# Second layer's V in nine products instead of twelve, with the keys of a pair's first batch rotated

## The reference

```python
def _L1_xattn_ref(x, context, Wq, Wk, Wv, Wk_ip, Wv_ip, Wo, bo):
    HEADS, DIM_HEAD, TEXT_LEN, IMG_SCALE = 16, 64, 77, 1.0
    ctx_txt = context[:, :TEXT_LEN, :]
    ctx_img = context[:, TEXT_LEN:, :]
    q = (x @ Wq).reshape(B, N, HEADS, DIM_HEAD)
    k = (ctx_txt @ Wk).reshape(B, TEXT_LEN, HEADS, DIM_HEAD)
    v = (ctx_txt @ Wv).reshape(B, TEXT_LEN, HEADS, DIM_HEAD)
    out = _attend(q, k, v)
    k_ip = (ctx_img @ Wk_ip).reshape(B, Li, HEADS, DIM_HEAD)
    v_ip = (ctx_img @ Wv_ip).reshape(B, Li, HEADS, DIM_HEAD)
    out_ip = _attend(q, k_ip, v_ip)
    out = out + IMG_SCALE * out_ip
    return out @ Wo + bo
```

## Time and profile before

| | us |
|---|---|
| median of 3 runs | 666.07 (665.52 to 667.85) |
| profiled execution | 668.6 |
| its span in the trace | 666.9 |
| TensorE busy | 612.9 |
| VectorE busy | 492.2 |
| ScalarE busy | 464.8 |
| GpSimd busy | 308.2 |

### The profile page before, as it was taken

How to read it: one execution, slowest core, us unless ns; L and a number is a source line. 1 busy time by engine, 2 the same in 40 slices (tenths; PEclk the granted TensorE clock), 3 DMA queues, 4 the chain that set the end, 5 groups by cost and what they waited for, 6 DMA issues and landing times.

```text
span 666.9 us, 16387 instructions
## 1 busy us (share of the span) xinstructions
PE 612.9 (92%) x5665; PEld 560.3 (84%) x5665; DVE 492.2 (74%) x1255; ACT 464.8 (70%) x1347; POOL 308.2 (46%) x444
## 2 busy tenths in 40 slices
PE   5898999999999999999999999999999879989990
PEld 5787888988889899999989988888888868979990
DVE  6588787798887978888797986876655665656654
ACT  5987889988888896666666766667555354646762
POOL 4365344444444434354445343445265574456450
PEclk9998999999999999999999999999889798989995
DMA  9800000000000000336664020000000032112215
GB/s 221 260 2 1 1 1 1 2 2 2 1 2 2 2 17 2 128 79 125 124 123 93 25 57 1 1 2 2 1 21 25 21 103 57 49 57 65 70 51 198
DMA packets 49626, 33.33 MB, mean 50 GB/s; under 512 B 9524, under 2 KB 46104, under 8 KB 49544
## 3 DMA queue, kind: packets, MB, share of 16 engines
q1 hardware_dynamic: 47272, 27.61, 17.3%
q0 software_dynamic: 2272, 4.67, 2.1%
HBM read 17.64 MB, written 14.63 MB: 48 GB/s over the span
## 4 chain that ended last, share of the span: by engine, by line
PE 53%; issue 14%; DVE 11%; POOL 9%; ACT 8%; DMA 2%; SPq 0%; POOLq 0%; DVEq 0%; another core or an unknown queue 0%; ACTq 0%
PE ps_j L646 6%; PE ps_h L868 6%; PE ps_s L815 6%; PE ps_h L885 5%; PE ps_t L853 5%; PE ps_j L404 4%; ACT scores L1068 4%; PE ph L1811 4%; PE py L1822 3%; POOL probs L1625 3%; POOL xs_scratch L1736 3%; PE ps_j L405 3%; PE ps_j L406 3%; PE pf L676 2%; DVE sums L1361 1%
## 5 line engine op out<-in xcount | busy, mean ns | idle before, releaser
L1625 POOL TENSOR_TENSOR probs<-scores,rsums 128x308 f32<-128x308 f32 (+1 forms) x192 | 152.2, 807 | 202.4 <-DVE rsums L1369 202.1
L1068 ACT ACTIVATE scores<-scores,neg_max 128x128 f32<-128x128 f32 x256 | 91.7, 398 | 0.0
L1034 ACT ACTIVATE probsT<-ps_t 128x512 f32<-128x512 f32 x128 | 76.4, 597 | 18.5 <-PE ps_t L853 18.2
L853 PE MATMUL ps_t<-ident,probs 128*128 128x128 f32 x512 | 79.4, 278 | 5.5 <-POOL probs L1625 4.4
L1361 DVE TENSOR_REDUCE sums<-scores 128x4 f32<-128x308 f32 (+2 forms) x156 | 66.3, 459 | 23.2 <-ACT scores L1072 11.7
L909 ACT ACTIVATE QT<-ps_j 128x512 f32<-128x512 f32 x64 | 38.3, 598 | 51.9 <-PE ps_j L406 51.9
L868 PE MATMUL ps_h<-probsT,V 128*64 128x128 f32 x1024 | 71.1, 281 | 2.3 <-DVE x_sb L1111 2.3
L885 PE MATMUL ps_h<-Wo,headsT 128*128 128x128 f32 x512 | 69.8, 280 | 2.0 <-ACT headsT L1027 1.9
L853 PEld LDWEIGHTS ps_t<-ident,probs 128*128 128x128 f32 x512 | 60.4, 143 | 9.4 <-POOL probs L1625 7.3
L885 PEld LDWEIGHTS ps_h<-Wo,headsT 128*128 128x128 f32 x512 | 63.8, 196 | 3.4 <-ACT headsT L1027 3.4
L868 PEld LDWEIGHTS ps_h<-probsT,V 128*64 128x64 f32 x1024 | 55.6, 138 | 13.2 <-issue 11.7
(11 more groups left out here) (248 smaller groups left out, 1640.2 us busy)
## 6 DMA issues: line engine op xcount, KB each, us to landing
xs_scratch<-xs SPq DMA_DIRECT2D x8, 1032.0 KB, 8.3
xt<-xs_scratch SPq DMA_DIRECT2D x39, 64.5 KB
w1b<-in_L_ffn_w_dram SPq DMA_DIRECT2D x1, 2048.0 KB, 10.4
big_raw<-in_L_ffn_w_dram SPq DMA_DIRECT2D x8, 256.0 KB
ysum<-y_scratch SPq DMA_DIRECT2D x4, 512.0 KB, 5.3
Wo<-in_L_xattn_Wo_dram SPq DMA_DIRECT2D x2, 512.0 KB, 5.2
out_dram<-x_sb SPq DMA_DIRECT2D x4, 256.0 KB, 2.4
x_sb<-in_x_dram SPq DMA_DIRECT2D x3, 256.0 KB, 9.2
```

Of the source, the lines that this page charges most:

```text
L853: ins = nc.tensor.transpose(ps_pT[:, j * S:(j + 1) * S], probs[s % 2][:, j, :], ident[:, :])
L1034: nc.scalar.activation(probsT[(s - 2) % 4][:, :, :].rearrange("p h s -> p (h s)"), ps_pT[:, :], ACT.Copy).then_inc(SS["pT_copied"], 1)
L1068: ins = nc.scalar.activation(scores[s % 4][:, j, :], scores[s % 4][:, j, :], ACT.Exp, bias=neg_max[:, 0, s % 4, j:j + 1], **total)
L1625: ins = nc.gpsimd.tensor_tensor(probs[(s - 1) % 2][:, :, k0:k1], scores[r][:, :, k0:k1], rsums[:, r, i, :].rearrange("p (h a) -> p h a", a ...
```

## The change

The text is spread so that three of the four operands are filled. Operand 0 (`st[0][:, 0]`, weights Wv) now holds text keys 0 to 63 of batch 1 and text keys 13 to 76 of batch 0. Operand 1 (`st[0][:, 1]`, weights Wv_ip) holds the image keys of batch 0 in rows 0 to 50 and those of batch 1 in rows 77 to 127; operand 2 (`st[1][:, 0]`, weights Wv) the 13 text keys of each batch that are left, in rows 51 to 76. Operands 1 and 2 add up in one half of the bank (six products), operand 0 makes the other half (three): nine products a block. In V, batch 0 then has its keys rotated (51 image keys, then 77 text keys), batch 1 in the old order.

ScalarE's V copy becomes three copies: rows 0 to 63 of both halves at once (512 columns), and rows 64 to 127 of each half by itself (256 columns), since the halves are swapped there. POOL writes the probabilities rotated for batch 0: one operation for all text keys (308 elements a row), and one for the image keys of each batch (102 each), three instead of two. The staging has 12 copies (of 13, 51 or 64 elements) instead of 4 (of 154 or 102), and at the turn to the second layer 6 memsets stand instead of 4. The first layer's code does what it did.

```diff
@@ project_v (TensorE)
-                for bb in range(PAIR):
-                    dst = bank[:, bb * 256:(bb + 1) * 256]
+                if lay == 0:
+                    parts = [[(0, 0, WV[0][0])], [(0, 1, WV[0][0])]]
+                else:
+                    parts = [[(1, 0, WV[1][0]), (0, 1, WV[1][1])], [(0, 0, WV[1][0])]]
+                for half, terms in enumerate(parts):
+                    dst = bank[:, half * 256:(half + 1) * 256]
                     n = 0
-                    for i, (w_hi, w_lo) in enumerate(WV[lay]):
+                    for i, c, (w_hi, w_lo) in terms:
                         for st, w in ((st_lo, w_hi), (st_hi, w_lo), (st_hi, w_hi)):
-                            ins = nc.tensor.matmul(dst, st[i][:, bb, :], w[:, cols], start=(n == 0),
-                                                   stop=(n == 3 * len(SEGS[lay]) - 1))
+                            ins = nc.tensor.matmul(dst, st[i][:, c, :], w[:, cols], start=(n == 0),
+                                                   stop=(n == 3 * len(terms) - 1))
                             n += 1
                 ins.then_inc(SS["v_ready"], 1)
@@ step (ScalarE), odd steps of layer 1
-                        nc.scalar.activation(V[hb % 2][:, :, :].rearrange("p b d -> p (b d)"),
-                                             v_bank(m)[:, :], ACT.Copy).then_inc(SS["v_copied"], 1)
+                            nc.scalar.activation(V[hb % 2][0:HALF, :, :].rearrange("p b d -> p (b d)"),
+                                                 v_bank(m)[0:HALF, :], ACT.Copy)
+                            for b in range(PAIR):
+                                ins = nc.scalar.activation(V[hb % 2][HALF:P, b, :],
+                                                           v_bank(m)[HALF:P, (1 - b) * 256:(2 - b) * 256], ACT.Copy)
+                        ins.then_inc(SS["v_copied"], 1)
@@ stage (POOL), layer 1
-                for i, (k0, k1) in enumerate(SEGS[lay]):
-                    for st, src in ((st_hi, ctxT_hi), (st_lo, ctxT_lo)):
-                        ins = nc.gpsimd.tensor_copy(st[i][:, :, k0:k1],
-                                                    src[:, bass.ds(g, 1), k0:k1, :].rearrange("p g s b -> p (g b) s"))
+                        for i, c, k0, k1, at, b in ((0, 0, 0, HALF, 0, 1), (0, 0, MIXED, TEXT, HALF, 0),
+                                                    (1, 0, 0, MIXED, IP, 0), (1, 0, HALF, TEXT, HALF, 1),
+                                                    (0, 1, TEXT, S, 0, 0), (0, 1, TEXT, S, TEXT, 1)):
+                            ins = nc.gpsimd.tensor_copy(st[i][:, c, at:at + k1 - k0], src[:, g, k0:k1, b])
@@ new function (POOL), called by step in place of the loop over SEGS for layer 1
+            def scale_rotated(dst, src, inverse):
+                by_b = src[:, :, :].rearrange("p (t b) k -> p t b k", b=PAIR)
+                inv = inverse.rearrange("p i (t b a) -> p i t b a", b=PAIR, a=1)
+                text = dst[:, :, :].rearrange("p (t b) k -> p t (b k)", b=PAIR)[:, :, IP:IP + PAIR * TEXT]
+                nc.gpsimd.tensor_tensor(text.rearrange("p t (b k) -> p t b k", b=PAIR), by_b[:, :, :, 0:TEXT],
+                                        inv[:, 0, :, :, :].broadcast_to([P, TILES, PAIR, TEXT]), ALU.mult)
+                for b, at in ((0, 0), (1, TEXT)):
+                    ins = nc.gpsimd.tensor_tensor(
+                        dst[:, :, :].rearrange("p (t b) k -> p t b k", b=PAIR)[:, :, b, at:at + IP],
+                        by_b[:, :, b, TEXT:S], inv[:, 1, :, b, :].broadcast_to([P, TILES, IP]), ALU.mult)
+                return ins
```

More of the change, by code:

```diff
@@ L312, in build_program @@
         SEGS = [[(0, S)], [(0, TEXT), (TEXT, S)]]
+        HALF, IP = S // 2, S - TEXT
+        MIXED = TEXT - HALF
         def l1w(name):
@@ L1060, in step @@
                         wait_pos(act, SS["heads_ready"], m - 1)
-                        nc.scalar.activation(V[hb % 2][:, :, :].rearrange("p b d -> p (b d)"),
-                                             v_bank(m)[:, :], ACT.Copy).then_inc(SS["v_copied"], 1)
+                        if lay == 0:
+                            ins = nc.scalar.activation(V[hb % 2][:, :, :].rearrange("p b d -> p (b d)"),
+                                                       v_bank(m)[:, :], ACT.Copy)
+                        else:
+                            nc.scalar.activation(V[hb % 2][0:HALF, :, :].rearrange("p b d -> p (b d)"),
[4 more added lines that the diff above has]
+                        ins.then_inc(SS["v_copied"], 1)
                     if lay == 0:
@@ L1593, in stage @@
                     pool.wait_ge(s_ctx_lo, part_of(g) + 1)
-                for i, (k0, k1) in enumerate(SEGS[lay]):
-                    for st, src in ((st_hi, ctxT_hi), (st_lo, ctxT_lo)):
-                        ins = nc.gpsimd.tensor_copy(st[i][:, :, k0:k1],
-                                                    src[:, bass.ds(g, 1), k0:k1, :].rearrange("p g s b -> p (g b) s"))
+                for st, src in ((st_hi, ctxT_hi), (st_lo, ctxT_lo)):
+                    if lay == 0:
+                        ins = nc.gpsimd.tensor_copy(st[0][:, :, :],
+                                                    src[:, bass.ds(g, 1), :, :].rearrange("p g s b -> p (g b) s"))
+                    else:
+                        for i, c, k0, k1, at, b in ((0, 0, 0, HALF, 0, 1), (0, 0, MIXED, TEXT, HALF, 0),
+                                                    (1, 0, 0, MIXED, IP, 0), (1, 0, HALF, TEXT, HALF, 1),
+                                                    (0, 1, TEXT, S, 0, 0), (0, 1, TEXT, S, TEXT, 1)):
+                            ins = nc.gpsimd.tensor_copy(st[i][:, c, at:at + k1 - k0], src[:, g, k0:k1, b])
                 ins.then_inc(SS["ctx_staged"], 1)
@@ L1623, in step @@
                     wait_pos(pool, SS["pT_ready"], n - 2)
-                    for i, (k0, k1) in enumerate(SEGS[prev if s == 0 else lay]):
-                        ins = nc.gpsimd.tensor_tensor(probs[(s - 1) % 2][:, :, k0:k1], scores[r][:, :, k0:k1],
-                                                      rsums[:, r, i, :].rearrange("p (h a) -> p h a", a=1)
-                                                      .broadcast_to([P, HB, k1 - k0]), ALU.mult)
+                    if (prev if s == 0 else lay) == 0:
+                        ins = nc.gpsimd.tensor_tensor(probs[(s - 1) % 2][:, :, :], scores[r][:, :, :],
+                                                      rsums[:, r, 0, :].rearrange("p (h a) -> p h a", a=1)
+                                                      .broadcast_to([P, HB, S]), ALU.mult)
+                    else:
+                        ins = scale_rotated(probs[(s - 1) % 2], scores[r], rsums[:, r, :, :])
                     ins.then_inc(SS["probs_ready"], 1)
@@ L1673, in step @@
                         for st in (st_hi, st_lo):
-                            nc.gpsimd.memset(st[0][:, :, TEXT:S].bitcast(F32), 0.0)
-                            nc.gpsimd.memset(st[1][:, :, 0:TEXT].bitcast(F32), 0.0)
+                            nc.gpsimd.memset(st[0][:, 1, IP:TEXT].bitcast(F32), 0.0)
+                            nc.gpsimd.memset(st[1][:, 0, 0:IP].bitcast(F32), 0.0)
+                            nc.gpsimd.memset(st[1][:, 0, TEXT:S].bitcast(F32), 0.0)
                     stage(G + 1, 0 if nxt != lay else g + 1, nxt)
```

## The result

The changed kernel took 678.71 us (674.19 to 680.85, four runs), the kernel before 665.8 us (664.5 to 667.85, four runs beside it): a ratio of 1.0173 with a 95% interval of [1.0137, 1.0209]. It is 11.5 us **slower** by the ratio (0.0173 x 665.8); the medians alone differ by 12.9 us. I had forecast 3.2 us faster, in a range that ended at 667.0. The sign, the forecast and the range are wrong.

A forecast was written before the change was run, and what follows sets the result against it. TensorE was taken to bound 26 V blocks, mostly not the six behind: 4.3 us gained less 1.2 in the tail, say 3.2; 666.07 - 3.2 = 662.9 us, range 657.0 to 667.0 (8 in 10).

The forecast's parts named there:

- TensorE, 0.35 us a block: In each V block, three products fewer at 0.117 us each save 0.35 us; 9.1 us in 26 blocks if TensorE decides everywhere.
- Inside VectorE's pieces the V blocks give nothing: Where the chain of waits runs on VectorE, six V blocks gain nothing: 6 x 0.35 = 2.1 us lost.
- main stretch: Second layer's first 26 V blocks, about 249 to 472 us, where TensorE mostly decides; forecast 4.3 us gained.
- The price of the copies, 0.54 us: On ScalarE, the two additional V copies of 256 columns cost 0.54 us a block; partitions taken as free.
- 5 x 0.54 = 2.7: Copies cost only at three `turn_d` (384, 426, 442 us) and two gate tanh (325, 409 us): 2.7 us lost.
- 9.1 - 2.7 - 2.1: For the 26 blocks: products' gain less copies' cost at five places and blocks beside VectorE's pieces, 4.3 us gained.
- ScalarE's odd step decides nearly everywhere: Rival: each of 32 V blocks costs 0.19 us, 6 us slower, 672 us; chance 0.08.
- The signs: Trace signs: `turn_d` idle 0.5 us longer, Wo product waiting for `headsT` over four times, POOL's three operations 1.3 us together.
- POOL's third operation, 0.1 us and hidden: Third probability operation adds 0.1 us a step, hidden until 487 us, then 12 steps cost 1.2 us.
- the rival of POOL blocked there: From 487 us, VectorE blocks POOL's third operation: 0.64 us in 12 steps, 7.7 us lost, 670.6 us; chance 0.07.
- Staging, 0.9 us more, hidden: POOL's twelve smaller staging copies take 0.9 us more, seven times; covered before V's next block, so nothing lost.
- The clock: Shorter V blocks could add a stretch of fallen TensorE clock; a half-clock block costs 0.84 us, either way, no place named.

The follow-up runs named there:

- nine_only: Kernel before with three of twelve products of each V block left out, nothing else changed: 651.7 us against 660.9, ratio 0.9873; repeated, 0.9859.
- copies_only: Kernel before with V copied in three pieces (rows 0 to 63, then rows 64 to 127 twice), twelve products kept: 675.2 us against 660.9, ratio 1.0199.
- after_one_copy: Changed kernel with V copied whole in one instruction, two halves left swapped: 660.9 us against 665.42 for the kernel before, ratio 0.9936.
- probs_only: Kernel before with POOL's probabilities in three operations, not rotated, all else as before: 659.68 us against 660.9, ratio 0.9983.
- after_v_late: Changed kernel with the second layer's three V copies moved behind the copy of the odd step's transposed probabilities: ratios 0.9886 and 0.9934 to the kernel before.
- nine_probs: Kernel before with three products of each V block left out and POOL's probabilities in three operations, not rotated: 659.9 us against 664.07, ratio 0.9942.

## Why the prediction was wrong, point by point

- **TensorE, 0.35 us a block**: right. The pitch of 0.117 us is what was saved, 0.36 us in the traces.
- **"Inside VectorE's pieces the V blocks give nothing", -2.1 us**: right in size. 9.1 - 2.1 = 7.0 us were forecast for the products without the copies, and the main stretch of nine_only is 7.0 and 6.4 us shorter. Its whole gain, 8.4 and 9.4 us, has 1.4 to 3.0 us more behind that, where I had 0.57 for the products; no run tells where.
- **The price of the copies, 0.54 us**: mis-sized; 0.77. I had added pitches of instructions on all partitions. Between the halves of the partitions there is no overlap, and this trace had no row of it. I had given the bound below, half of 0.50 saved, and none above: a second bound was wanted, that nothing overlaps, which by the durations of the earlier trace rows is 0.60 + 2 x 0.38 = 1.36 us up to the exp, 0.86 more than before. My own sign of being wrong was a second or third copy of more than 0.35 us: they take 0.37.
- **Where the copies count, "5 x 0.54 = 2.7"**: the term is mis-sized more than the list of places is wrong. The five places are there and cost 5.4 us in copies_only, 0.9 to 1.6 each, where the price of 0.77 would give 3.9. Not on the list were the pair from 459 us (2.3) and two from 358 us (0.7). The main stretch lost 8.6 us for 2.7 forecast. Behind it 0.54 us were forecast, and 13.2 - 8.6 leaves some 4.6, with the spread of single traces named above.
- **The sum "9.1 - 2.7 - 2.1"**: this is the step that failed most. I added the gain and the cost as if each kept its worth beside the other, and took the blocks outside the five places as giving their 0.35 us with three copies as with one. That a place isn't in the chain doesn't say how far it is from it. Alone, the products give 7.0 us and the copies take 8.6; together the stretch is 9.0 us longer. Of the 7.4 us between sum and whole, 3.6 are missing already in after_one_copy, 1.5 are the pair at half clock, and the rest are not placed by a run. The 13.3 us between the forecast of 4.3 gained and the 9.0 lost are so 5.9 us of the copies' term and 7.4 us of a gain that didn't survive.
- **The slower rival, ScalarE's odd step decides nearly everywhere**, held at 8%: it names the right queue, and it isn't what happened either. By its own sum with the measured price it gives 32 x (0.77 - 0.35) = 13.4 us slower, near the 11.5 measured; this is luck. In the main stretch ten of 26 pairs are longer, by up to 3.3 us, seven are shorter and nine the same. What I held against it, that the odd step's transposes wait for the even step's copy, is true and beside the point: VectorE's sums wait for the odd exp.
- **The signs**: `turn_d` idle longer (0.92 us at one place, 0.5 expected), eight waits for `headsT` instead of four, and POOL's three operations at 1.34 us came as written. They show the mechanism, and say nothing of its size.
- **POOL's third operation, 0.1 us and hidden**: right alone (0.9983; from 320.14 the three take 1.34 us, 0.15 above the pair of before), wrong beside nine products, where the transfers that POOL waits for pace it. In the tail it cost nothing that probs_only shows, and the rival of POOL blocked there fell with it.
- **Staging, 0.9 us more, hidden**: right alone (0.9994; the twelve take 2.1 us). With the ring tight it brings longer holdups of VectorE. The Trainium skill ("SBUF — State Buffer", "Who interferes with whom") has VectorE and GpSimd share a port; I used the rule for POOL as the loser only. Here VectorE is the loser, and for the sum of POOL's next operations (2.70 us for L1175, which reads two tiles; 0.90 is usual).
- **The clock**: the mean was 0.969 before and 0.965 after, 0.980 in nine_only. In the main stretch it cost some 1.5 us at one place of the changed kernel, behind 1.99 us of idle time, and nothing before or in copies_only, where it is 1.00 throughout. I had named this risk without a place. It comes and goes: of the two traces of after_v_late one has it there (220.2 us) and one hasn't (218.1).

What stays open: the 7 to 8 us between the sum of the parts and the whole are only in part measured by runs; and what lies behind the main stretch, where the stretch from the last scores to the end takes 124 to 132 us in the traces of the several kernels, in no order that I can explain.

## What to carry to other kernels

Before you pay on one engine for a gain on another, work out the paying engine's slack at every place where it recurs, not only at those where the chain already runs through it, and hold the cost and the gain together against it: here most places bore the cost alone, and few bore both. Ask also whether the new work must stand where the old did; here the same three copies cost 13 us in front of the exp and about 0.3% a few instructions later. And price a split instruction in both directions, by columns and by partitions, since only one of them was cheap.

## What the runs showed of the hardware

- On ScalarE an instruction whose partitions start elsewhere than those of the one ahead started only when that had ended (0.60 us after a 64x512 copy); one that starts at the same partition started inside it (0.47 to 0.50 us, also from 128 rows to 64). 64 partitions cost what 128 do: 0.58 and 0.60 us.
- Behind 1.99 us of idle time TensorE's granted clock was 0.71 in the mean of 5.9 us; 16 products of the heads then took 1.91 us, and 1.02 at full clock.
- Splitting a copy of 512 columns in three by columns cost 0.10 us (0.60 to the next start, not 0.50).
- A VectorE operation of 0.17 us took 1.84 us while GpSimd ran several operations without a gap, and ended 0.03 us behind the last of them.
- The transfers that clear an expert's slots took 8.1 to 8.5 us each in the two shown of nine_probs (1,032 KB each), and with one in each pair of steps they paced a kernel that was otherwise ready for less.
